# Column means of the first projection from a scale column and the raw weights, centred weights in six parts

## What is computed

```python
p = _layernorm(p, ln1_g, ln1_b)            # (x - mean) * rsqrt(var + eps) * g + b
y = jnp.einsum('bnd,de->bne', p, W_proj)   # 768 -> 192
return _layernorm(y, ln2_g, ln2_b)
```

## Time and profile before

| | us |
|---|---|
| median of 3 runs | 141.26 (140.8 to 141.6) |
| the profiled execution | 140.0 |
| its span in the trace | 138.0 |
| PE busy | 115.0 (83%) |
| DVE busy | 88.9 (64%) |
| ACT busy | 69.0 (50%) |
| POOL busy | 67.0 (49%) |

### The profile page before, as it was taken

The page is one execution under the profiler, slowest core; times in us unless marked ns, Lnnn a source line. Parts: engine busy times, 40 slices in busy tenths (PEclk is TensorE's granted clock), DMA queues, the critical chain, the costliest instruction groups (busy, mean ns, idle before and its releaser), DMA issues.

```text
span 138.0 us, 4819 instructions
## 1 busy us (share of the span) xinstructions
PE 115.0 (83%) x1779; PEld 93.6 (68%) x1779; DVE 88.9 (64%) x380; ACT 69.0 (50%) x234; POOL 67.0 (49%) x158
## 2 busy tenths in 40 slices
PE   0297799999699999999999999997986860999920
PEld 0297799888377868578787796866964630788700
DVE  0211999999643687985857558586987440159980
ACT  3000004242862848648675686846644468763553
POOL 8500277767847428837265382743664000007871
PEclk9999999999999999999999999999999555599995
DMA  1999899988000000000000000000000000000232
GB/s 14 337 293 278 269 305 320 314 319 214 5 7 0 5 0 7 5 0 7 0 5 5 0 5 0 10 5 0 5 0 7 0 0 0 5 0 24 72 89 71
DMA packets 7677, 10.34 MB, mean 75 GB/s; under 512 B 2056, under 2 KB 5032, under 8 KB 7656
## 3 DMA queue, kind: packets, MB, share of 16 engines
q1 hardware_dynamic: 7656, 10.06, 24.2%
HBM read 9.17 MB, written 0.88 MB: 73 GB/s over the span
## 4 chain that ended last, share of the span: by engine, by line
PE 47%; DVE 22%; issue 12%; POOL 10%; ACT 4%; DMA 3%; SPq 1%; POOLq 1%; DVEq 0%; ACTq 0%
DVE st L649 8%; PE ps L565 7%; PE ps L436 6%; PE ps L476 5%; PE ps L496 3%; PE ps L542 3%; PE ps L399 3%; DMA wt<-in_w_tok 3%; PE ps L489 3%; PE ps L519 3%; DVE y L663 3%; PE ps L578 3%; DVE st L671 2%; PE ps L507 2%; PE ps L407 2%
## 5 line engine op out<-in xcount | busy, mean ns | idle before, releaser
L417 PE MATMUL ps<-wc,xT 128*108 128x192 f32 (+1 forms) x132 | 23.0, 327 | 1.5 <-DVE wc L637 1.5
L940 ACT ACTIVATE hT<-ps,b,g 96x108 f32<-96x108 f32 (+1 forms) x22 | 8.4, 430 | 27.9 <-PE ps L426 27.9
L417 PEld LDWEIGHTS ps<-wc,xT 128*108 128x108 f32 (+1 forms) x132 | 20.7, 170 | 2.0 <-DVE wc L637 1.8
L436 PE MATMUL ps<-wqk,hT 96*108 96x384 f32 (+1 forms) x44 | 16.2, 490 | 0.7 <-ACT qp L962 0.7
L1125 POOL TENSOR_SCALAR pw<-mv 108x1 f32<-108x1 f32 (+1 forms) x11 | 3.7, 337 | 21.3 <-DVE mv L780 21.3
L476 PE MATMUL ps<-hT,wv 96*128 96x108 f32 (+1 forms) x88 | 12.5, 284 | 0.0
L1139 POOL TENSOR_SCALAR var<-mv 108x1 f32<-108x1 f32 (+1 forms) x11 | 2.4, 223 | 18.9 <-DVE mv L875 18.4
L950 ACT ACTIVATE sq<-ps 108x384 f32<-108x384 f32 (+1 forms) x11 | 5.4, 490 | 12.4 <-PE ps L436 12.4
L476 PEld LDWEIGHTS ps<-hT,wv 96*128 96x128 f32 x88 | 10.7, 191 | 0.7
L649 DVE BATCH_NORM_STATS2 st<-xs 108x6 f32<-108x384 f32 (+1 forms) x22 | 10.9, 540 | 0.2 <-issue 0.2
L960 ACT ACTIVATE km<-ps,imgsel 108x192 f32<-108x192 f32 (+1 forms) x32 | 11.0, 418 | 0.0
(11 more groups left out here) (106 smaller groups left out, 304.6 us busy)
## 6 DMA issues: line engine op xcount, KB each, us to landing
xT<-in_x_t SPq DMA_DIRECT2D x10, 324.0 KB, 7.0
xs<-in_x SPq DMA_DIRECT2D x10, 324.0 KB
out<-o SPq DMA_DIRECT2D x10, 81.0 KB
wt<-in_w_tok SPq DMA_DIRECT2D x1, 576.0 KB, 4.2
wqk<-in_w_qk SPq DMA_DIRECT2D x1, 288.0 KB, 8.7
xT<-in_x_t SPq DMA_DIRECT2D x1, 216.0 KB, 7.5
xs<-in_x SPq DMA_DIRECT2D x1, 216.0 KB
wv<-in_w_v SPq DMA_DIRECT2D x1, 192.0 KB, 9.0
```

Of the source, the lines that this page charges most:

```text
L417: mm = pe.matmul(tokp(g), xT[:, o + kc * n:o + (kc + 1) * n], wc[:, kc, :], start=kc == 0, stop=kc == KC - 1)
L436: mm = pe.matmul(qkp(g), hT[:, f, t0:t0 + tokens(g)], wqk[:, f, :, :, :].rearrange("p j h d -> p (j h d)"), start=f == 0, stop=f == 1)
L940: ins = act.activation(hT[:, f, t0:t0 + tokens(g)], htp(g)[:, f, :], ACT.Identity, bias=b2[:, f:f + 1], scale=g2[:, f:f + 1])
```

## The change

1. Scale and offset come in one transfer (`gb1`), and the weights in two transfers of half the chunks each, with a semaphore each; the host lays them out so that a partition's data of a half is one contiguous piece.
2. The means are computed from W itself: PE uses as stationary operand the scale column divided by 768 (`gs1`, one small DVE instruction), so `wg`, its six DVE instructions, `share` and the POOL memset that fills it are gone. The products b @ W no longer stand in front.
3. The centred weights are made in six DVE instructions (W * g - mean), each with its own signal; `token(0)` waits for them one by one.
4. b @ W stands behind `token(0)` on PE, and its copy behind the first group's statistics on DVE.

```diff
-            sp.dma_start(g1[:, :], ln1_g).then_inc(ln1_in, 16)
-            sp.dma_start(b1[:, :], ln1_b).then_inc(ln1_in, 16)
-            sp.dma_start(wt[:, :, :], w_tok.rearrange("(k p) e -> p k e", p=128)).then_inc(wtok_in, 16)
+            sp.dma_start(gb1[:, :, :].rearrange("p t k -> p (t k)"), ln1_gb).then_inc(ln1_in, 16)
+            for i in range(2):
+                k0 = i * KC // 2
+                sp.dma_start(wt[:, k0:k0 + KC // 2, :].rearrange("p k e -> p (k e)"),
+                             w_tok[:, k0 * D:(k0 + KC // 2) * D]).then_inc(wtok_in[i], 16)
...
+            def column_means():
+                pe.wait_ge(gs1_ready, 1)
+                for kc in range(KC):
+                    if kc % (KC // 2) == 0:
+                        pe.wait_ge(wtok_in[kc // (KC // 2)], 16)
+                    mm = pe.matmul(csp(), gs1[:, kc:kc + 1].broadcast_to([128, 128]), wt[:, kc, :],
+                                   start=kc == 0, stop=kc == KC - 1)
+                mm.then_inc(csp_ready, 1)
...
-            def column_means():
-                pe.wait_ge(share_set, 1)
-                for kc in range(KC):
-                    pe.wait_ge(wg_ready, kc + 1)
-                    mm = pe.matmul(csp(), share[:, :], wg[:, kc, :], start=kc == 0, stop=kc == KC - 1)
-                mm.then_inc(csp_ready, 1)
...
                 for kc in range(KC):
+                    if g == 0:
+                        pe.wait_ge(wc_ready, kc + 1)
                     mm = pe.matmul(tokp(g), xT[:, o + kc * n:o + (kc + 1) * n], wc[:, kc, :],
                                    start=kc == 0, stop=kc == KC - 1)
...
-            offset()
             column_means()
-            pe.wait_ge(wc_ready, 1)
             for g in range(P1):
                 token(g)
+                if g == 0:
+                    offset()
...
+            def mean_shares():
+                dve.wait_ge(ln1_in, 16)
+                dve.tensor_scalar(gs1[:, :], gb1[:, 0, :], 1.0 / PD, None, ALU.mult).then_inc(gs1_ready, 1)
+
             def token_weights():
-                dve.wait_ge(ln1_in, 32)
-                dve.wait_ge(wtok_in, 16)
+                dve.wait_ge(csp_ready, 1)
                 for kc in range(KC):
-                    dve.tensor_scalar(wg[:, kc, :], wt[:, kc, :], g1[:, kc:kc + 1], None,
-                                      ALU.mult).then_inc(wg_ready, 1)
-                dve.wait_ge(wg_ready, KC)
-                dve.wait_ge(csp_ready, 1)
-                dve.tensor_tensor(wc[:, :, :], wg[:, :, :], csp().unsqueeze(1).broadcast_to([128, KC, D]),
-                                  ALU.subtract).then_inc(wc_ready, 1)
+                    dve.scalar_tensor_tensor(wc[:, kc, :], wt[:, kc, :], gb1[:, 0, kc:kc + 1], csp(),
+                                             ALU.mult, ALU.subtract).then_inc(wc_ready, 1)
+
+            def token_offset():
                 dve.wait_ge(bwp_ready, 1)
                 dve.tensor_copy(bw[:, :], bwp()).then_inc(bw_ready, 1)
                 dve.wait_ge(bw_ready, 1)
...
+            mean_shares()
             token_weights()
             x_stats(0)
             x_moments(0)
+            token_offset()
...
-            pool.memset(share[:, :], 1.0 / PD).then_inc(share_set, 1)
```

More of the change, by code:

```diff
@@ L62, in tokens, with build @@
     return images(g) * TOK
-def build(nc, x, x_t, w_tok, ln1_g, ln1_b, ln2_g, ln2_b, g2col, b2col, w_qk, w_v, w_proj, b_proj, temp, slots, scale,
+def build(nc, x, x_t, w_tok, ln1_gb, ln2_g, ln2_b, g2col, b2col, w_qk, w_v, w_proj, b_proj, temp, slots, scale,
           w_down, b_down, w_up, b_up, ident_h, imgsel_h, negmask_h, out):
@@ L78, in build @@
         negmask = sb("negmask", [128, GI * SL])
-        g1 = sb("g1", [128, KC])
-        b1 = sb("b1", [128, KC])
+        gb1 = sb("gb1", [128, 2, KC])
+        gs1 = sb("gs1", [128, KC])
         wt = sb("wt", [128, KC, D])
-        wg = sb("wg", [128, KC, D])
         wc = sb("wc", [128, KC, D])
         bw = sb("bw", [128, D])
-        share = sb("share", [128, 128])
         g2 = sb("g2", [F, 2])
@@ L242, in build @@
         ln1_in = sem("ln1_in")
-        wtok_in = sem("wtok_in")
+        wtok_in = [sem(f"wtok_in{i}") for i in range(2)]
         ln2_in = sem("ln2_in")
@@ L260, in build @@
         sp_ready = sem("sp_ready")
-        share_set = sem("share_set")
-        wg_ready = sem("wg_ready")
+        gs1_ready = sem("gs1_ready")
         csp_ready = sem("csp_ready")
@@ L394, in _ @@
         def _(pe):
+            def column_means():
[6 more added lines that the diff above has]
+                mm.then_inc(csp_ready, 1)
             def offset():
-                pe.wait_ge(ln1_in, 32)
-                pe.wait_ge(wtok_in, 16)
                 for kc in range(KC):
-                    mm = pe.matmul(bwp(), b1[:, kc:kc + 1].broadcast_to([128, 128]), wt[:, kc, :],
+                    mm = pe.matmul(bwp(), gb1[:, 1, kc:kc + 1].broadcast_to([128, 128]), wt[:, kc, :],
                                    start=kc == 0, stop=kc == KC - 1)
                 mm.then_inc(bwp_ready, 1)
-            def column_means():
-                pe.wait_ge(share_set, 1)
-                for kc in range(KC):
-                    pe.wait_ge(wg_ready, kc + 1)
-                    mm = pe.matmul(csp(), share[:, :], wg[:, kc, :], start=kc == 0, stop=kc == KC - 1)
-                mm.then_inc(csp_ready, 1)
             def token(g):
@@ L1197 @@
          .reshape(128, KC * tokens(g)) for g in range(NG)], axis=1)
-    arrays["in_w_tok"] = w["tok_W_proj"]
-    arrays["in_ln1_g"] = w["tok_ln1_g"].reshape(KC, 128).T
-    arrays["in_ln1_b"] = w["tok_ln1_b"].reshape(KC, 128).T
+    arrays["in_w_tok"] = w["tok_W_proj"].reshape(KC, 128, D).transpose(1, 0, 2).reshape(128, KC * D)
+    arrays["in_ln1_gb"] = np.stack([w["tok_ln1_g"], w["tok_ln1_b"]]).reshape(2 * KC, 128).T
     arrays["in_ln2_g"] = w["tok_ln2_g"]
```

## The result

| | before | changed |
|---|---|---|
| median of 4 runs, us | 141.43 (140.8 to 141.6) | 145.40 (143.8 to 145.9) |
| span of the profiled execution, us | 138.0 | 143.2 |
| ratio | | 1.042 (95% interval 1.033 to 1.051) |

I had forecast 140.0 us, in a range of 139.2 to 141.2. The kernel became 4.2% slower. (Executions of one kernel lie up to some us apart here; a ratio is formed over the undisturbed executions alone, so a kernel with too few of them has a median and a range and no ratio.)

What follows compares the result with a forecast made beforehand. The prediction took the opening's chain to y(0), then DVE at 2.2 us a group, as the bound. Second statistics at 14.75 instead of 16.00 gain 1.25 us; the median of 141.26 becomes 140.0 us, range 139.2 to 141.2.

Steps and rivals of the forecast that it cites:

- Does the data keep up?: Opening, rows of group 4: they land at about 21.1 us, needed at 21.35; cost zero, at most 0.5 us.
- D: Rival: the opening shortens but the time does not follow, through row landings or the clock's low stretch; 141.2 us, chance 0.11.
- The sign that I had named: Named as proof of error: DVE waits for `xs` in the stage, PE starts later than 5, or records exceed 500 ns after 11.
- PE's start: Opening: PE's first product at 4.55 us, bounds 3.9 to 5.5, instead of 5.96.
- The half's landing: Opening: the first half of the weights, issued at 1.19 us, needs 3.2 us and lands at 4.4.
- The means done: Opening, PE: six products at the low rate, 4.2 us, give the means at 8.75 us; before, 13.1.
- the copy as the late step: Opening: DVE waits some 2 us for b @ W, whose copy delays the second statistics to 14.75 us instead of 16.00.
- PE's rate rise 6.0 us after its first product: Opening, PE: products go from 0.66 to 0.35 us each at 10.55 us, so b @ W is complete at 14.15.
- rival B: PE's rate rises before `token(0)`, or the half lands at 3.9 us; gain capped at 1.5 us, 139.75 us, chance 0.15.
- Rival C: PE's 0.55 us pause before `token(0)` restarts the time to the rate rise, moving it to 15.3; 142.3 us, chance 0.06.
- The forecast of 1.25 us: Opening: second statistics and y(0) come 1.25 us earlier and the shift reaches the end; gain of 0.9 to 1.4 us, chance 0.50.
- The cap of 1.5 us: Stage after the opening: the landing of `xs` of group 4 limits any gain to about 1.5 us.

Runs made afterwards that it cites:

- j2: Kernel before, with the weights fetched as two transfers of three chunks each, both waited for, PE and DVE work unchanged: median 145.8 us, no ratio.
- e4: Changed kernel with scale and offset again as two arrays and two transfers, the weights' large pieces kept: 138.8 us once and 145.8 us once.
- i1: Changed kernel with an unused 32-byte tile ahead of `xs`, so `xs` and `xT` start at multiples of 64: median 144.0 us, no ratio.
- j1: Changed kernel's new order on PE and DVE, with transfers, input arrays and tile addresses as before the change: median 140.0 us, ratio 1.012 (1.000 to 1.023).
- f4: Kernel before with six buffers for the rows instead of four: median 140.5 us, ratio 1.003 (0.995 to 1.011).
- g2: Kernel before with scale and offset in one input array, still fetched by two transfers: median 142.9 us, ratio 1.025 (1.016 to 1.035).
- e1: Kernel before with the weights laid out by the host as one contiguous 4608-byte piece a partition, still one transfer: 139.1 and 160.7 us.
- e3: Changed kernel with the weights in their old layout, three 768-byte pieces a partition in each half transfer: median 145.2 us, ratio 1.039 (1.034 to 1.044).
- f3: Kernel before with 112 rows loaded a group (80 for the last) instead of 108 (72): median 140.2 us, ratio 1.000 (0.995 to 1.006).
- i3: Kernel before with an unused 32-byte tile, so `xs` and `xT` start 32 bytes past a multiple of 64: 140.7 us, ratio 0.985 (0.962 to 1.008).

## Why the prediction was wrong, point by point

**Where it failed.** The step "Does the data keep up?" took the landings of the kernel before, moved them 0.47 us forward for the earlier start of the stream, and concluded that `xs` of group 4 would be there at 21.1. In fact they landed at 25.62 and the statistics of group 4 started at 25.64. The premise under it, never written out, was that the pace of a stream is set by its bytes and that cutting a transfer at its head leaves the pace of all later ones alone. j2 shows that it does not: 238 for 284 GB/s from 10 to 20 us, and 4.4 us lost by the attention stage. I had costed the cut as a gain of 1.0 us of landing and nothing else, and asked of it only whether its second half comes in time. No rival covered it: D let the landing eat the gain, at 141.2, but not more than the gain. A sentence on the transfers should have had a bound on its other side: with 1.0 us of slack on `xs` (itself an estimate, between two landings), a pace a fifth slower over some 20 us of stream is worth about 4 us by estimate, and the view that showed the backlogs of 6 to 9 us was in front of me. The sign that I had named, DVE waiting for `xs` in the stage, is what came true.

**Steps that held** (forecast first). PE's start, 4.55 against 4.50. The half's landing: 3.2 us against a median of 3.3 in the issues of the profile:

```profile
wt<-in_w_tok SPq DMA_DIRECT2D x2, 288.0 KB, 3.3
```

The fit of the Trainium skill (DMA: Bandwidth & Descriptors, section "Anatomy of one DMA"), which gave an estimate of 2.7 for it, was below this trace, as it was for the whole transfer. The means done at 8.75 against 8.5; the first part 0.45 us later against 0.56 (PE's first token product at 9.06); PE never waiting between the parts; the copy as the late step, with DVE waiting some 2 us for it against 1.51. Two small ones did not hold: the scaling of six columns took 0.43 us, above my bound of 0.32, without effect, since it was done before the weights were there; and SP issued `xs` of group 4 at 14.88 and not at 12.9, because it was still busy with the transfers ahead of it, `xT` of group 4 last (13.65 to 14.83).

**A term mis-sized, and not a constant.** The forecast let PE's rate rise 6.0 us after its first product. In the profiled execution of the changed kernel it rose earlier, as in rival B. The records of L399 have a median of 528 ns between 6 and 7 us, and of the last three, starting from 7.5 to 8.1, one took 327,

```profile
L399 PE MATMUL ps<-wt,gs x5: 527/528/528, 5.6 to 6.9; 128*128 128x192 f32 x5
...
L399 PE MATMUL ps<-wt,gs x3: 327/471/528, 7.5 to 8.1; 128*128 128x192 f32 x3
```

so near 8 us, some 3.6 us after the first product. The twelve records of `token(0)` then took 2.17 us, and the gain at y(0) was 2.45 us and not 1.25. That was the luck of one execution. The same kernel profiled again (g4) ran `token(0)` at the low rate and had its first record below 400 ns at 13.3, 9.0 us after its first product at 4.23; its y(0) came at 16.82, a gain of 0.43:

```profile
9.01 4.15 PE L418 MATMUL ps<-wc,xT 128*108 128x192 f32 x12 [0.60 <-DVE wc L637]
...
16.82 0.37 DVE L665 SCALAR_TENSOR_TENSOR y<-ps,rstd,bw 108x192 f32<-108x192 f32 x1
```

Over all twenty traces the first such record comes 3.0 to 6.2 us after the first product in the old opening, and in the new one after 3.0 to 3.6 us (five traces), after 4.8 (four) or after 9.0 to 9.4 (three: e4, g4, i1). So the 6.0 us read from one trace was one draw of many. Rival C is not out: in the three late ones the pause of 0.60 us fell while the records were still slow, which is C's condition. But the rate rose at 13.3 to 14.0 and not at 15.3, and in the four traces of 4.8 us it rose right after such a pause, so that the pause delays it is not shown. In j1 the rise came early, 3.3 us after the first product at 6.08, so its y(0) is the case of an early rise.

**What the opening is worth.** The forecast of 1.25 us rested on DVE as the bound of the stage. j1 tells what it was worth with a stream like that of before: nothing that can be measured (1.012, 1.000 to 1.023), and its trace points at the stream as a second bound right behind DVE. Two other comparisons of single traces fit it: y(0) came 2.02 us earlier in the changed kernel's first trace than in g4 and its group 4 still 0.81 us later (25.64 and 24.83), and in f4 (old opening, six buffers) y(0) came 1.35 us earlier than before and the attention stage at 34.29, as before. The cap of 1.5 us that I gave was the right thought and too large. It assumed the stream's best pace, and in j1's profile it was 284 and not 315 GB/s from 20 us on.

## What to carry to other kernels

When a stage has a second bound a microsecond behind the first, a gain on the first is worth at most about that microsecond, and an edit that also touches the second has to be costed there first. Transfers issued back to back are one stream: its pace is itself a measured quantity, which a cut at its head changed here by 12 to 20%, so such a cut should be tried by itself, in the unchanged kernel, before anything is built on it. If a change bundles a new order of work with new transfers, the two halves run apart (j1 and j2) tell in one comparison what a dozen theories about the bundle don't. And where a forecast leans on the moment of a change of rate, read that moment from several executions: one trace gave 2.45 us of gain at y(0) and the next 0.43, for the same kernel.

## What the runs showed of the hardware that I had not expected

- Fetching 576 KB of weights as two transfers and not one slowed the 6 to 7 MB of transfers behind them from 284 to 238 GB/s (10 to 20 us) and from 315 to 251 GB/s (20 to 30 us), at nearly the same busy share of the transfer engines (0.99 and 1.04, 0.92 and 0.91; j2 against before, which ran on another chip; j1, on j2's chip and with one transfer, moved 286 and 284).
- The same two 3 KB transfers out of one array and not out of two made the same kernel 2.5% slower (g2); why is open.
- Things that cost nothing that these runs can tell: pieces of 4608 for 768 bytes (e1, one execution, and e3), a backlog of up to 14.8 us (f4), 108 or 112 rows (f3), targets 32 bytes past a multiple of 64 (i3).
- With late data PE's granted clock can fall within its busiest stage: it read 0.50 from 26 to 32 us in the changed kernel's first trace, but 1.00 throughout in g4, the same kernel with much the same pauses. By the attention stage the two are 0.35 us apart.
- The rise from 1.2 to 2.4 GHz after PE's first product came 3.0 to 9.4 us after it over twenty traces, and 3.6 and 9.0 us after it in two of the same kernel (changed, g4).
